# A first attention stage whose TensorE work is cut into 64x32 tiles, with each half of a block on its own half of the array

## The reference, cut to what matters

```python
x = L0_attn_x                                   # 2 batches x 1024 rows x 128
x = x + layernorm(attn(layernorm(x)))           # first stage: 16 heads of width 8, with a bias
x = x + layernorm(ffn(layernorm(x)))            # ffn: a second attention (16 heads), then a mixture of 8 experts

def attn(x):
    k, v, q = heads(x @ w_in.T)
    logits = einsum('bhld,bhmd->bhlm', q, k) / sqrt(8) + bias[head][l - m]
    return einsum('bhlm,bhmd->bhld', softmax(logits), v)
```

## Time and profile before

| | us |
|---|---|
| median of 3 runs | 910.42 (909.69 to 911.81) |
| the profiled execution | 909.28, its span 907.4 |
| PE busy | 807.3 (89%) |
| DVE busy | 752.4 (83%) |
| ACT busy | 636.9 (70%) |
| POOL busy | 242.8 (27%) |

### The profile page before, as it was taken

One profiled execution on the slowest core, in us unless ns is written; L12 is line 12 of the kernel. 1 busy time (PEld: TensorE's weight loads), 2 busy tenths in 40 slices (PEclk: granted clock), 3 DMA queues, 4 the chain that ended last, 5 costly groups with the idle time before them and its releaser, 6 DMA issues.

```text
span 907.4 us, 22092 instructions
## 1 busy us (share of the span) xinstructions
PE 807.3 (89%) x8629; PEld 302.8 (33%) x8629; DVE 752.4 (83%) x1196; ACT 636.9 (70%) x1266; POOL 242.8 (27%) x548
## 2 busy tenths in 40 slices
PE   4289999999999999999999999999999999954950
PEld 2023333333333333333332223322232322244950
DVE  5589877989999998879999998899999899236735
ACT  6037777777776777777778988899989899921311
POOL 4110423200000405322300552342101301004773
PEclk9569999999999999999999999999999999966985
DMA  3655534655556445445313343232312121101313
GB/s 99 202 166 177 171 109 155 195 166 164 165 171 191 134 152 174 132 156 178 107 54 107 109 126 92 79 110 73 96 54 61 55 90 49 32 9 50 51 51 100
DMA packets 69469, 104.67 MB, mean 115 GB/s; under 512 B 15845, under 2 KB 45861, under 8 KB 69365
## 3 DMA queue, kind: packets, MB, share of 16 engines
q1 hardware_dynamic: 62805, 68.31, 25.8%
q10 hardware_dynamic: 5088, 31.92, 9.9%
q0 software_dynamic: 1472, 3.02, 1.5%
HBM read 84.19 MB, written 18.87 MB: 114 GB/s over the span
## 4 chain that ended last, share of the span: by engine, by line
PE 68%; DVE 9%; POOL 6%; DMA 5%; issue 4%; ACT 4%; SPq 2%; POOLq 0%; DVEq 0%
PE bank L1286 23%; PE bank L1305 20%; PE bank L1312 12%; PE bank L1266 7%; DVE unit_max L1003 4%; ACT prob_mem L901 4%; POOL prob_mem L791 3%; POOL moe_out L797 2%; DMA maxima_rows<-max_rows 2%; PE bank L1349 2%; PE bank L1239 2%; DVE stats L946 1%; PE bank L1234 1%; DMA q_rows<-maxima_rows 1%; DMA bias_parts<-prob_mem 1%
## 5 line engine op out<-in xcount | busy, mean ns | idle before, releaser
L901 ACT ACTIVATE prob_mem<-bank 128x512 f32<-128x512 f32 x1024 | 556.7, 597 | 140.2 <-PE bank L1312 116.5
L1266 PE MATMUL bank<-k_rows,q_rows 56*128 56x512 bf16 x1024 | 326.3, 392 | 20.9 <-DMA k_rows<-k_parts 12.4
L1305 PE MATMUL bank<-q_rows,k_rows 59*128 59x512 bf16 x1024 | 332.6, 386 | 6.2 <-DMA q_rows<-maxima_rows 2.3
L999 DVE CUSTOM_DVE_ANT_1 no_use<-bank,w_moe 128x1024 bf16<-128x1024 f32 x256 | 305.7, 1219 | 31.7 <-PE bank L1266 29.3
L1286 PE MATMUL bank<-prob_mem,v_ring 128*32 128x256 f32 x4096 | 320.5, 386 | 7.7 <-issue 6.6
L1003 DVE TENSOR_REDUCE unit_max<-bank 128x1 f32<-128x1024 f32 x256 | 297.3, 1216 | 16.3 <-PE bank L1266 14.7
L702 POOL CAST max_parts<-unit_max 128x8 bf16<-128x8 f32 x64 | 12.3, 192 | 557.4 <-DVE unit_max L999 315.2
L1305 PEld LDWEIGHTS bank<-q_rows,k_rows 59*128 59x128 bf16 x1024 | 80.9, 93 | 236.7 <-issue 109.5
L1286 PEld LDWEIGHTS bank<-prob_mem,v_ring 128*32 128x32 f32 x4096 | 102.6, 109 | 152.8 <-ACT prob_mem L901 62.6
L1312 PE MATMUL bank<-skew_mem,pick 96*32 96x512 bf16 x1664 | 138.2, 389 | 0.0
L1010 DVE TENSOR_TENSOR bank<-bank,w_moe 128x512 f32<-128x512 f32 x96 | 67.0, 698 | 25.0 <-PE bank L1305 24.7
(11 more groups left out here) (177 smaller groups left out, 526.9 us busy)
## 6 DMA issues: line engine op xcount, KB each, us to landing
w_moe<-bias_rows ACTq DMA_DIRECT2D x31, 960.0 KB, 5.4
q_rows<-q_parts SPq DMA_DIRECT2D x252, 48.0 KB
k_rows<-k_parts SPq DMA_DIRECT2D x126, 96.0 KB
skew_mem<-bias_parts SPq DMA_DIRECT2D x32, 378.0 KB, 4.4
unit_sums<-o_ring SPq DMA_DIRECT2D x63, 128.0 KB, 2.3
w_moe<-in_L_ffn_w_dram SPq DMA_DIRECT2D x16, 256.0 KB, 3.0
q_parts<-prob_mem SPq DMA_DIRECT2D x8, 384.0 KB, 3.1
k_parts<-prob_mem SPq DMA_DIRECT2D x24, 128.0 KB, 2.7
```

Source lines behind the costliest of these rows:

```text
L901: nc.scalar.activation(prob[:, kb, half * N:(half + 1) * N], b_bank(("exp", exp_no(n, kb, half))), ACT.Exp).then_inc(exp_done, 1)
L999: nc.vector.tensor_tensor_reduce(out=no_use[:, qb % 2, :].rearrange("p (k c) -> p k c", k=QB), in0=scores.rearrange("p (k c) -> p k c", k= ...
L1266: return nc.tensor.matmul(sa_slot(QB * m + qb)[:, f, :], q_rows[rows, m % SLOTS, qb * P:(qb + 1) * P], k_rows[rows, m % SLOTS, f * N:(f + ...
L1305: return nc.tensor.matmul(b_bank(("exp", exp_no(n, kb, f))), k_rows[rows, n % SLOTS, kb * P:(kb + 1) * P], q_rows[rows, n % SLOTS, f * N:( ...
```

## The change

In the first stage (units 0 to 31 as B; the A scores of units 2 to 33):

- **Scores** of a half are four matmuls of 32 output partitions on the half f's 64 rows of the array (`half_b`, `half_a`: 64x32 tiles), in place of one with 128 output partitions.
- **Bias** of half f lies on that half's rows too: `skew` holds 16 shifts times 3 parts (48 rows) for each half instead of 32 times 3, and is read twice, at columns 16 apart (`bias_b` with part 0 and 1), with `pick` in two forms. DVE no longer adds any bias (`add_bias` goes).
- **Values** are split by keys: keys 0 to 63 on the lower half of the array into bank `AV`, keys 64 to 127 on the upper into `AV_UPPER` (`weigh_half`). ACT copies both banks at once (512 columns in place of 256), and POOL adds the two (`add_sums`), before SP stores the sum.
- **Maxima** are taken over 512 columns, twice a block, from three single banks (`SA_HALF`) instead of two slots of two; one small DVE operation joins the halves at the unit's end. Their transposition is two matmuls of 64 columns, the second one block later, and ACT copies the result between the exponentials of block 3.
- **Order**: half 1's A scores go beside half 0's B scores at a block's start; half 1's B scores follow half a block later, and the two halves' values lie at different places.
- `skew` is loaded by two transfers instead of one.

```diff
-        SB = [bank[:, 4 + n, :] for n in range(3)]
-        AV = bank[:, 7, 0:W]
+        SA_HALF = [bank[:, n, :] for n in range(3)]
+        SB = [bank[:, 5 + n, :] for n in range(3)]
+        AV_UPPER, AV = bank[:, 3, 0:W], bank[:, 4, 0:W]
...
-            src = bass.AP(row.tensor, row.offset, [[1, 32], [2 * L, 3], [1, SKW]])
-            queue.dma_start(skew[0:96, n % 3, 0:SKW], src).then_inc(skew_loaded[n % 3], 16)
+            for f in range(2):
+                src = bass.AP(row.tensor, row.offset + f * N, [[1, SHIFTS], [2 * L, 3], [1, SKW]])
+                queue.dma_start(skew[f * HP:f * HP + SR, n % 3, f * N:f * N + SKW], src).then_inc(skew_loaded[n % 3], 16)
...
+            def add_sums(n):
+                pool.wait_ge(o_copied, n + 1)
+                if n >= 2:
+                    pool.wait_ge(o_stored[n % 2], 16 * (n // 2))
+                nc.gpsimd.tensor_tensor(o_ring[:, n % 2, :], o_halves[:, n % 2, 0, :], o_halves[:, n % 2, 1, :], ALU.add).then_inc(o_summed, 1)
...
+            def half_b(n, kb, f):
+                b_bank_free(("exp", exp_no(n, kb, f)))
+                rows = slice(f * HP, f * HP + KR + 3)
+                for c in range(4):
+                    at = kb * P + VM * c
+                    nc.tensor.matmul(b_bank(("exp", exp_no(n, kb, f)))[VM * c:VM * (c + 1), :], k_rows[rows, n % SLOTS, at:at + VM],
+                                     q_rows[rows, n % SLOTS, f * N:(f + 1) * N], start=True, stop=False,
+                                     tile_position=(f * HP, VM * c))
...
+            def bias_b(n, kb, f, part):
+                rows = slice(f * HP, f * HP + SR)
+                for c in range(4):
+                    at = f * N - kb * P + VM * c + L - P + SHIFTS * part
+                    ins = nc.tensor.matmul(b_bank(("exp", exp_no(n, kb, f)))[VM * c:VM * (c + 1), :], pick[rows, part, :],
+                                           skew[rows, n % 3, at:at + N], start=False, stop=(part == 1), tile_position=(f * HP, VM * c))
...
+                    half_b(n, kb, 0)
+                    half_a(m, kb, 1)
+                    if kb == MAX_AT + 1:
+                        pe.wait_ge(max_t_lower, n + 1)
+                        maxima_half(n + 1, 1).then_inc(max_t_mm, 1)
+                    bias_b(n, kb, 0, 0)
+                    if value[1] == 0:
+                        half_b(n, kb, 1)
+                        bias_b(n, kb, 0, 1)
+                        bias_b(n, kb, 1, 0)
+                        half_a(m, kb, 0)
+                        bias_b(n, kb, 1, 1)
+                        value_ready(value[0], value[1])
+                        weigh_half(value[0], value[1], 0)
+                        weigh_half(value[0], value[1], 1)
+                    else:
+                        value_ready(value[0], value[1])
+                        if value[0] >= 0:
+                            weigh_half(value[0], value[1], 1)
+                        bias_b(n, kb, 0, 1)
+                        half_a(m, kb, 0)
+                        half_b(n, kb, 1)
+                        bias_b(n, kb, 1, 0)
+                        if value[0] >= 0:
+                            weigh_half(value[0], value[1], 0)
+                        bias_b(n, kb, 1, 1)
```

275 lines of the change are left out of this document (177 added, 98 removed).

## The result

The changed kernel takes 927.06 us (median of 4 runs, 922.46 to 929.4) against 910.58 for the kernel before on the same chip (4 runs): a ratio of 1.0177, 95% interval 1.0142 to 1.0213. It is slower by 16.5 us, where 17.5 less was predicted. Its profiled execution has a span of 927.2 us.

The account below looks back on a forecast made before the run. PE, busy 89% of the span, was taken to bound the kernel. 24 gained less 2, 3 and 1.5 gave 17.5 off the profiled 909.3, so 891.8; with 1.1 for the median, 893 us, range 868 to 912.

Parts of the forecast that it names:

- PE cannot be fed: Rival: 96 PE instructions a block come too slowly, over 0.016 us each; 1010 or 1280 us; chance 0.11.
- Maxima's way: Maxima's trip through DRAM: late in about four units where SP is late, 0.7 us each; lost 3 (0 to 12).
- Plain units 11.5 us: First-stage units without side work take 11.5 us instead of 12.25; 24.0 us gained over 32 units.
- The slot: PE's time for one group of 512 columns in one half of the array: taken as 0.22 us.
- the halves run side by side: PE's two array halves work at once, so a unit's work is 48 slots, 10.56 us against 11.5.
- the bank ring: PE's waits for banks around blocks 1 to 3: 2.6 slots lost at block 3, 1.65 at block 4.
- 4.25 slots: Bank waits added to a unit's 48 slots of PE work, giving 11.5 us.
- DVE's share: Sign: DVE's busy share stays below PE's, falling from 11.2 to about 10.1 us a unit.
- my two bounds: DVE's maximum over 512 columns: between 0.57 and 0.67 us, taken as 0.61.
- Side work: 38 first-stage pieces each bring one more change of shape, 0.09 us: up to 3.4 us, lost 2.
- Passage to the second stage: Last two blocks' values wait for the last exponentials, their copy precedes the next stage's first exponential: lost 1.5.
- The weights: Rival: PE's weight loads are not hidden, groups 0.31 us apart, +114, 1023 us; chance 0.04 with overlap failing otherwise.

Follow-up runs that it names:

- a_notab: The changed kernel with the 960 KB bias table loaded for the first four units alone (stale tables, wrong output): 903.3 us, ratio 0.9912 to the kernel before.
- b_notab: The kernel before with the bias table loaded for the first four units alone (stale tables, wrong output): 909.6 us, ratio 0.9990.
- b_split: The kernel before with first-stage scores as four matmuls of 128 columns and biases as two of 256: 917.4 us, ratio 1.0072.
- a_wide: The changed kernel with each half's scores in one matmul of 128 output partitions again: 1005.8 us, ratio 1.1054 to the kernel before.
- a_halfp4_sp: The changed kernel with a bfloat16 table in four pieces of 32 whole rows, and SP's skewed-table transfers moved after the maxima's load: 904.8 us.
- b_sp: The kernel before with SP's order changed: maxima out, sums' store, maxima in, then the skewed table: 910.6 us, ratio 0.9993.

## Why the prediction was wrong

**The step that failed** is the last sentence on the rival "PE cannot be fed": "The instructions' own transfers, 69 of 16 KB at 0.5% of 16 engines' span, 1.05 us each, are no bound: 256 instructions last 3.5 us." I compared 3.5 us with a transfer's duration, 1.05. What counts is how late it starts (up to 5.0 us behind the table, 1.4 in the median), plus its 1.05, plus 1.2 to 1.5 until PE goes on. Before, there were late starts too, up to about 4 us, and pieces of 10 us hid them all. The runs put it at 18 us of stalls and 3.4 us of half clock (half of the two stretches of 3.4 us behind stalls). a_notab shows it: 24 us back, of which 17.5 are stalls and 3.4 the clock. b_notab, b_split and a_wide are on the other side: where a piece lasts 5 us or more, the same table costs 0.9 us of stalls at the most. The rival itself was priced for another mechanism, a steady rate per instruction, and that one was refuted: in a steady block PE took 0.215 to 0.22 us for 16 instructions, under 0.014 each.

**Maxima's way: lost 3 (0 to 12).** Mechanism right, size off: the waits are 9.6 us in place of 1.2, 2.7 to 3.8 in each of three units, where I charged four of 0.7. SP's program grew by one issue a unit, PE's unit got shorter, and where SP also loads weights, loads sums or stores parts, it sends the maxima late (4.6 us behind their copy at 297.38). SP's new order gives 8 us back.

**Plain units 11.5 us: right** (11.48), where nothing stalls. The slot is 0.215 to 0.22, the halves run side by side, the bank ring waits at blocks 3 and 4 (0.25 and 0.44 us beyond a slot, 0.69 in all for my 4.25 slots, 0.93). DVE's share stayed below PE's; its maximum over 512 columns took 0.67 (331.5 us for 496), the upper of my two bounds and not the 0.61 that I took, so 10.7 us a unit, still under 11.5.

**Side work: lost 2.** A unit with four pieces takes 14.27 us after (copies at 131.54, 145.79 and 160.07) for 14.55 before, so it gains 0.28 where a plain one gains 0.77. That is 0.12 a piece, 4.7 us over 38: more than the 3.4 I gave as the most.

**Passage to the second stage: lost 1.5.** Not there: the unit across it takes 10.6 us, 0.4 less than before.

**The weights** are hidden, as the rows said. The Trainium skill has a rule in "TensorE: Matmul & The Clock Gate", the section on packing small matmuls by row and column tiling, that a load overlaps only with matmuls on another row group. By my working from the rows that would have given groups 0.31 apart; here four loads and four matmuls of one group follow those of another on the same rows at 0.215. The trace does not agree with it.

The sum, in the stage: the rest fell by 11.6 (409.0 to 397.4), the stalls cost 17.9, the maxima 8.4, the clock 3.7: +18.4, which is 436.6 less 418.2. Of the clock's 3.7 not all is the stalls': two of the four stretches lie behind waits for the maxima, and the start of the stage has less of the lower level than before. With the table and SP's lateness out of the way the rest fell by 16.4 and the kernel took 896.7, 4 us above the predicted 893. **A version that beats both kernels** is a_halfp4_sp: 904.8 us, 0.9940 of before (0.9916 to 0.9963). The kernel before was not run with the smaller table; without any table from unit 4 on (b_notab), or with SP's order (b_sp), it gains nothing.

## What to carry to other kernels

Count the instructions of an engine that a change makes denser: 256 of them are one transfer that stands in line with all data, and the time that they last has to cover its late start, its duration and more than a microsecond after it (here 5 us was enough but for 0.9 us in all, and 3.5 to 4.2 was not). A gap put down to issue that cuts a group of like instructions in two, at the same place of every 256, is this; a large transfer beside it is the first thing to shrink, and here four pieces of long rows did better than one piece or four of short rows. And a unit that gets shorter shortens the time of every queue that serves it: look at the queue that issues most, in its fullest unit, before the gain is booked.

## What the runs showed of the hardware

- An instruction transfer of 16 KB takes 1.05 us, but starts up to 5.0 us late while a 960 KB transfer and others hold the engines 88% of the time; PE goes on 1.2 to 1.5 us after its end.
- After an idle time of 2.3 us up to 244.52 PE's clock was granted at half for 3.4 us from 245.6 on, which costs about 1.7 us more than the stall's own length (an estimate: half the stretch). Only one other of the 18 stalls was followed by this, and the longest was not.
- Four matmuls and loads of 64x32 tiles on each half of the array, bf16 and two-pass fp32 in turn, start 0.215 us after the last four: under 0.014 us an instruction, both halves together. A change between 128 and 32 output partitions costs 0.10 to 0.12 us each time.
- The same 480 KB a unit took 6.9% of the engines in rows of 3840 bytes and 9.0% in rows of 960.
